# Logits of seven of the eight key heads from float32r halves in three terms, in a one-core attention and feed-forward block

## The reference

```python
q = apply_rope((layernorm(x) @ Wq).reshape(b, t, 32, 128)).reshape(b, t, 8, 4, 128)
k = apply_rope((ctx @ Wk).reshape(b, t, 8, 128))
v = (ctx @ Wv).reshape(b, t, 8, 128)
logits = jnp.einsum('btkgd,bTkd->bkgtT', q, k) * 0.0883883
logits = 30 * jnp.tanh(logits / 30)
weights = softmax(where(mask, logits, -1e30))
x = x + einsum('bkgtT,bTkd->btkgd', weights, v).reshape(b, t, 4096) @ Wo
# then: NF4-quantise and dequantise w1, w2, w3 (blocks of 64)
h = silu(layernorm(x) @ dq1.T) * (layernorm(x) @ dq2.T)
x = x + h @ dq3.T
```

## Time and profile before

| | |
|---|---|
| time, median of 3 runs | 800.66 us (799.59 to 801.32) |
| profiled execution | 800.16 us, of which the span is 798.3 us |
| TensorE busy | 789.0 us, 99% |
| VectorE busy | 661.7 us, 83% |
| ScalarE busy | 547.4 us, 69% |
| GpSimd busy | 367.3 us, 46% |
| granted TensorE clock | 9 (full) in all 40 slices |

### The profile page before, as it was taken

One profiled execution on the slowest core, in us unless ns is written; L12 is line 12 of the kernel. 1 busy time (PEld: TensorE's weight loads), 2 busy tenths in 40 slices (PEclk: granted clock), 3 DMA queues, 4 the chain that ended last, 5 costly groups with the idle time before them and its releaser, 6 DMA issues.

```text
span 798.3 us, 10879 instructions
## 1 busy us (share of the span) xinstructions
PE 789.0 (99%) x3810; PEld 635.9 (80%) x3810; DVE 661.7 (83%) x741; ACT 547.4 (69%) x859; POOL 367.3 (46%) x210
## 2 busy tenths in 40 slices
PE   8999999999999999999999999999999999999998
PEld 6777887878887788878888888888778888888876
DVE  6897755898999999898988889899574999999913
ACT  6467737787877868678787788786643877868510
POOL 4773265446637457366465365473100534435010
PEclk9999999999999999999999999999999999999999
DMA  9636456333432433425235335231401031412022
GB/s 335 199 129 201 131 155 169 110 99 93 139 107 77 154 97 112 129 71 171 79 84 152 92 93 165 80 103 47 136 14 40 27 126 54 124 28 76 14 69 106
DMA packets 60981, 87.56 MB, mean 110 GB/s; under 512 B 6272, under 2 KB 29952, under 8 KB 60928
## 3 DMA queue, kind: packets, MB, share of 16 engines
q1 hardware_dynamic: 59744, 84.06, 35.7%
q10 hardware_dynamic: 1184, 2.82, 1.0%
HBM read 51.00 MB, written 19.07 MB: 88 GB/s over the span
## 4 chain that ended last, share of the span: by engine, by line
PE 85%; DVE 6%; issue 5%; ACT 2%; DMA 1%; POOL 0%; POOLq 0%; SPq 0%; DVEq 0%
PE bank L530 7%; PE prjs L514 7%; PE prjs L516 7%; PE bank L532 7%; PE bank L531 7%; PE prjs L515 7%; PE bank L590 7%; PE avp L618 6%; PE trp L503 4%; PE bank L496 3%; PE bank L498 3%; PE bank L497 3%; PE prjs L498 2%; PE prjs L496 2%; PE prjs L497 2%
## 5 line engine op out<-in xcount | busy, mean ns | idle before, releaser
L1294 POOL TENSOR_TENSOR qT<-cs_loop,sw 128x512 f32<-128x512 f32 x56 | 107.2, 1915 | 183.4 <-DMA sw<-cs_loop 176.1
L514 PE MATMUL prjs<-xh,wqh 128*128 128x512 f32 x256 | 123.3, 482 | 0.0
L530 PE MATMUL bank<-woh,ath 128*128 128x512 f32 x256 | 100.8, 394 | 1.0 <-DVE atl L1161 0.9
L516 PE MATMUL prjs<-xh,wql 128*128 128x512 f32 x256 | 100.2, 391 | 0.0
L532 PE MATMUL bank<-woh,atl 128*128 128x512 f32 x256 | 99.9, 390 | 0.0
L531 PE MATMUL bank<-wol,ath 128*128 128x512 f32 x256 | 99.7, 389 | 0.0
L862 ACT ACTIVATE ath<-trp 128x512 fp32r<-128x512 f32 x64 | 38.2, 596 | 89.5 <-PE trp L503 89.5
L515 PE MATMUL prjs<-xl,wqh 128*128 128x512 f32 x256 | 99.5, 389 | 0.0
L995 DVE TENSOR_TENSOR cs_loop<-prjs,csq 128x1024 f32<-128x1024 f32 x56 | 68.3, 1220 | 21.4 <-PE prjs L516 21.2
L987 DVE SCALAR_TENSOR_TENSOR nfv<-nfq,nfv 128x1408 f32<-128x1408 uint8 x42 | 79.1, 1883 | 0.2
L850 ACT ACTIVATE nrm<-avp,rs 128x128 f32<-128x128 f32 x256 | 72.6, 372 | 7.0 <-DVE rs L1148 6.7
(11 more groups left out here) (187 smaller groups left out, 1966.6 us busy)
## 6 DMA issues: line engine op xcount, KB each, us to landing
sw<-cs_loop SPq DMA_DIRECT2D x112, 128.0 KB, 2.3
stage<-wq_pieces SPq DMA_DIRECT2D x32, 256.0 KB, 2.9
stage<-wo_pieces SPq DMA_DIRECT2D x32, 256.0 KB, 3.1
stage<-dq_scratch SPq DMA_DIRECT2D x32, 256.0 KB, 3.2
ks_scratch<-qT SPq DMA_DIRECT2D x16, 256.0 KB, 3.1
vs_scratch<-vst SPq DMA_DIRECT2D x16, 256.0 KB, 3.5
kcur<-ks_scratch SPq DMA_DIRECT2D x16, 256.0 KB, 2.9
vcur<-vs_scratch SPq DMA_DIRECT2D x16, 256.0 KB, 3.4
```

What stands on the lines that cost most here:

```text
L514: nc.tensor.matmul(o, wqh[:, g, k, :], xh[:, k, cs], start=k == 0, stop=False)
L516: last = nc.tensor.matmul(o, wql[:, g, k, :], xh[:, k, cs], start=False, stop=k == KT - 1)
L530: nc.tensor.matmul(o, ah, wh[:, g, :], start=g == 0, stop=False)
L1294: nc.gpsimd.tensor_tensor(dst, products(ru, slot)[:, 0, :], sw[:, slot, :], ALU.add).then_inc(roped, 1)
```

## The change

For key heads 1 to 7 (steps 8 to 63) the logits are made in three terms of float32r. Head 0 keeps float32, with its operands now in the tiles `kfirst` and `qfirst`. For every unit u from 8 on:

- GpSimd's `query_rope` writes the rotated query back into `cs_loop` (`roped_query(u)`) and not into `qT`;
- ScalarE makes its high part (`query_high`, into `qT`, now float32r), between exp and `high`;
- VectorE makes its low part (`query_low`, into `ql`), between `mask` and `rope_parts`.

The keys of the next head are loaded into `kraw`; ScalarE copies the high part to `kcur` in steps b = 2 and 6 (`key_high`) and GpSimd subtracts for the low part `klow` in steps b = 3 and 7 (`key_low`). `rope_parts` waits for the low part of the unit that held its slot. Tiles are placed anew, and a DMA scratch size is given to the builder.

```diff
             def logits(j):
...
-                if s == 0:
-                    pe.wait_ge(roped, NK + 8 * kv + 4 * h + 4)
-                    pe.wait_ge(k_in[h], 16 * kv + 16)
+                if s == 0 and kv == 0:
+                    pe.wait_ge(roped, NK + 4 * h + 4)
+                    pe.wait_ge(k_in[h], 16)
+                if s == 0 and kv > 0:
+                    pe.wait_ge(q_low_done, 8 * kv + 4 * h - 4)
+                    pe.wait_ge(k_low_done, 2 * kv + h - 1)
                 wait(pe, weights_done, j)
-                nc.tensor.matmul(lgp[:, :], kcur[:, h, s * 128:(s + 1) * 128],
-                                 qT[:, h, :, s * 128:(s + 1) * 128], start=True, stop=True).then_inc(logits_done, 1)
+                if kv == 0:
+                    nc.tensor.matmul(lgp[:, :], kfirst[:, h, ss], qfirst[:, h, :, ss],
+                                     start=True, stop=True).then_inc(logits_done, 1)
+                else:
+                    three(lgp[:, :], [(kcur[:, h, ss], klow[:, h, ss], qT[:, h, :, ss], ql[h][:, :, ss])])\
+                        .then_inc(logits_done, 1)
...
+            def query_high(u):
+
+                kv, half, g = unit_parts(u)
+                act.wait_ge(roped, NK + u + 1)
+                act.wait_ge(logits_done, 8 * (kv - 1) + 4 * half + 4)
+                nc.scalar.activation(qT[:, half, g, :], roped_query(u), ACT.Copy).then_inc(q_high_done, 1)
+
+            def key_high(kv, h):
+
+                act.wait_ge(k_in[h], 16 * kv + 16)
+                nc.scalar.activation(kcur[:, h, :], kraw[:, h, :], ACT.Copy).then_inc(k_high_done, 1)
...
                     if j + 3 < NSTEP:
                         weights(j + 3)
+                    if 8 <= j + 7 < NUNIT:
+                        query_high(j + 7)
                     if j + 2 < 8 * NKV - 8:
                         high(34 + j)
                     if j + 1 < NSTEP:
                         values(j + 1)
+                    if b in (2, 6) and not last:
+                        key_high(kv + 1, b // 4)
...
                 dve.wait_ge(proj_done, ru + 1)
-                wait(dve, roped, ru - 1)
+                if ru < NK + AHEAD + 2:
+                    dve.wait_ge(roped, ru - 1)
+                else:
+                    dve.wait_ge(q_low_done, ru - NK - AHEAD - 1)
...
+            def query_low(u):
+
+                kv, half, g = unit_parts(u)
+                dve.wait_ge(q_high_done, u - 7)
+                nc.vector.tensor_tensor(ql[half][:, g, :], roped_query(u), as_f32(qT[:, half, g, :]), ALU.subtract)\
+                    .then_inc(q_low_done, 1)
...
                     if j + 3 < NSTEP:
                         mask(j + 3)
+                    if 8 <= j + 7 < NUNIT:
+                        query_low(j + 7)
                     u = j + AHEAD
                     if u < NUNIT:
                         rope_parts(NK + u, u % 2, csq[:, :, :])
...
                 if u < 8:
                     pool.wait_ge(k_out[u], 32)
-                else:
-                    pool.wait_ge(logits_done, 8 * (kv - 1) + 4 * half + 4)
-                rope(NK + u, u % 2, qT[:, half, g, :])
+                rope(NK + u, u % 2, qfirst[:, half, g, :] if u < 8 else roped_query(u))
+
+            def key_low(kv, h):
+                pool.wait_ge(k_high_done, 2 * kv + h - 1)
+                nc.gpsimd.tensor_tensor(klow[:, h, :], kraw[:, h, :], kcur[:, h, :].bitcast(f32),
+                                        ALU.subtract).then_inc(k_low_done, 1)
...
+                    if b in (3, 7) and not last:
+                        key_low(kv + 1, b // 4)
                     if j + 2 < 8 * NKV - 8:
                         weight_low(34 + j)
                     if j + AHEAD < NUNIT:
...
-    nc = bacc.Bacc("TRN2", target_bir_lowering=False, num_devices=1)
+    nc = bacc.Bacc("TRN2", target_bir_lowering=False, num_devices=1, dynamic_dma_scratch_size=4096)
```

More of the change, by code:

```diff
@@ L98, in build @@
             wgl = sb("wgl", [128, 2, 2, KT, 128], f32r, ffn)
-        kcur = sb("kcur", [128, 2, 512])
+        with ExitStack() as first_head:
+            kfirst = sb("kfirst", [128, 2, 512], f32, first_head)
+        kcur = sb("kcur", [128, 2, 512], f32r)
         vcur = sb("vcur", [128, B, DH + 1])
@@ L103, in build @@
         eb = sb("eb", [128, 2, 512])
-        qT = sb("qT", [128, 2, G, 512])
+        with ExitStack() as first_head:
+            qfirst = sb("qfirst", [128, 2, G, 512], f32, first_head)
+        qT = sb("qT", [128, 2, G, 512], f32r)
         with ExitStack() as ffn:
@@ L127, in build @@
             nfx = sb("nfx", [128, CH], f32, loop)
+            ql0 = sb("ql0", [128, G, 512], f32r, loop)
         sb("ffn_place", [128, 6144])
@@ L136, in build @@
         wol1 = sb("wol1", [128, G, D], f32r)
+        ql1 = sb("ql1", [128, G, 512], f32r)
+        with ExitStack() as arriving:
+            kraw = sb("kraw", [128, 2, 512], f32, arriving)
+        klow = sb("klow", [128, 2, 512], f32r)
+        ql = [ql0, ql1]
         woh, wol = [woh0, woh1], [wol0, wol1]
@@ L177, in build @@
                                                     sem("h_lo"))
+        q_high_done, q_low_done = sem("q_high_done"), sem("q_low_done")
+        k_high_done, k_low_done = sem("k_high_done"), sem("k_low_done")
         mask_step, key_swapped = sem("mask_step"), sem("key_swapped")
@@ L209, in nf_stored, with roped_query @@
             return 32 + 16 * c if c <= NKV else 32 * (c - NKV) + 32 + 16 * NKV
+        def roped_query(u):
+            return cs_loop[:, u % 2, 0, :]
         def products(ru, slot):
@@ L354, in k_store @@
                 wait(sp, roped, u + 1)
-                sp.dma_start(ks_d[u % 8, u // 8], qT[:, u % 8 // 4, u % 4, :]).then_inc(k_out[u % 8], 16)
+                sp.dma_start(ks_d[u % 8, u // 8], qfirst[:, u % 8 // 4, u % 4, :]).then_inc(k_out[u % 8], 16)
             def head_piece(p):
@@ L389, in _ @@
                     wait(sp, consts, 2)
-                    sp.dma_start(kcur[:, 0, :], ks_d[0, 0]).then_inc(k_in[0], 16)
+                    sp.dma_start(kfirst[:, 0, :], ks_d[0, 0]).then_inc(k_in[0], 16)
                     sp.dma_start(vcur[:, 0:4, 0:DH], vs_d[0, 0]).then_inc(v_in[0], 16)
@@ L419, in head @@
                         wait(sp, logits_done, j + 3)
-                        sp.dma_start(kcur[:, b // 4, :], ks_d[kv + 1, b // 4]).then_inc(k_in[b // 4], 16)
+                        sp.dma_start(kraw[:, b // 4, :], ks_d[kv + 1, b // 4]).then_inc(k_in[b // 4], 16)
                     for c in nf_finished(j - 1):
@@ L441, in weights_in @@
                 sp.dma_start(stage[:, n % 4, :], dq12[:, col:col + D]).then_inc(piece_in[n % 4], 16)
-            sp.dma_start(kcur[:, 1, :], ks_d[0, 1]).then_inc(k_in[1], 16)
+            sp.dma_start(kfirst[:, 1, :], ks_d[0, 1]).then_inc(k_in[1], 16)
             sp.dma_start(vcur[:, 4:8, 0:DH], vs_d[0, 1]).then_inc(v_in[1], 16)
@@ L585, in logits @@
                 kv, h, s = j // B, j % B // 4, j % 4
-                if s == 0:
-                    pe.wait_ge(roped, NK + 8 * kv + 4 * h + 4)
-                    pe.wait_ge(k_in[h], 16 * kv + 16)
-                wait(pe, weights_done, j)
-                nc.tensor.matmul(lgp[:, :], kcur[:, h, s * 128:(s + 1) * 128],
-                                 qT[:, h, :, s * 128:(s + 1) * 128], start=True, stop=True).then_inc(logits_done, 1)
+                ss = slice(s * 128, (s + 1) * 128)
+                if s == 0 and kv == 0:
[4 more added lines that the diff above has]
+                    pe.wait_ge(k_low_done, 2 * kv + h - 1)
+                wait(pe, weights_done, j)
+                if kv == 0:
[4 more added lines that the diff above has]
+                        .then_inc(logits_done, 1)
             for v in range(16):
@@ L1332, in _ @@
                     pool.wait_ge(k_out[u - 8], 16)
-                key_rope(u, qT[:, u % 8 // 4, u % 4, :])
+                key_rope(u, qfirst[:, u % 8 // 4, u % 4, :])
                 if u < 6:
```

## The result

The changed kernel takes 837.99 us (median of 4 runs, 836.49 to 838.81) against 800.99 before: a ratio of 1.0468, 95% interval 1.0455 to 1.048, so 4.7% or 37 us slower. I had predicted 825 us with a range of 803 to 838: the direction and the rough size were right, but a third of the loss was missing, and the median lies at the very edge of the range. In the profiled executions 35.8 of the 38.7 us more fall between the first and the last `rope_parts` of the loop.

The account below looks back on a forecast made before the run. TensorE was taken to set the pace before, and a one-step loop through VectorE after. 24 - 1.9 - 0.7 + 4 = 25.4 us on the profiled 800.16 gave 825 us, range 803 to 838.

Parts of the forecast that it names:

- TensorE's gain: Logits on TensorE: three float32r matmuls replace the float32 call, saving 0.18 us a step, 10 us over 56 steps.
- the closed loop: `rope_parts`, swap, GpSimd's addition, `query_high`, `query_low`, next `rope_parts` form a one-step loop; likeliest case, 815 to 840 us, 74%.
- 7.45 us for a quiet step: Loop length in a quiet step, just under TensorE's 7.48, so lateness from heavy steps is not given back.
- 9.55 for the step with `nf_prepare`: VectorE works without idling in that interval, so its 8.95 us plus the subtraction becomes 9.55.
- the loop's price: Added time over the 55 `rope_parts` intervals from the closed loop: 19 to 28 us, middle 24.
- the lock: VectorE and GpSimd shut each other out of SBUF ports; charged only for 14 `key_low` ahead of `query_low`: 4 us of 0 to 18.
- 24 - 1.9 - 0.7: Loop's loss, less 1.9 us that `atl` may be late before TensorE stops, less 0.7 for steps 57 to 60.
- VectorE's work in it plus 0.60: Between two `rope_parts`, an interval lasts at least VectorE's former work plus the subtraction's 0.60 us.
- the locks pile up: Rival: ScalarE and GpSimd held behind late rotations, and `key_low` at its full 18 us; over 840 us, 5%.
- in a quiet step this costs nothing: ScalarE waiting in `query_high` for the rotation costs nothing in quiet steps, since the rotation is done before exp.
- rival two: VectorE is merely full: lateness is made up in quiet steps, each costing 7.57 to 7.7 us; 797 to 803 us, 12%.

Follow-up runs that it names:

- e8: Changed kernel without the queries' low part (no VectorE subtraction; logits lack that term) and with ScalarE's `query_high` behind its values: 793.93 us.
- e13: Changed kernel with `query_low` at its place but its second input in PSUM, and the mask's signal to TensorE moved to `query_low`: 814.13 us.
- e1: Changed kernel with `query_low` right behind the next unit's `rope_parts` instead of ahead of it, opening the one-step loop: 830.63 us.
- e6: Kernel before plus 56 VectorE subtractions of 128x512 behind the mask, both inputs in SBUF, result unused: 827.12 us.
- e7: Changed kernel with `query_low` behind `rope_parts` and ScalarE's `query_high` behind the values, all terms kept: 828.52 us.
- e3: Changed kernel without the queries' low part (no VectorE subtraction; the second matmul reads the high part again): 801.89 us.
- e14: e13 with `query_low` behind `rope_parts`, so neither one-step loop nor lock: 812.53 us.
- e16: e14 with ScalarE's `query_high` behind the values: 805.96 us.
- e9: Kernel before plus 56 VectorE subtractions of 128x512 ahead of the mask, one input in PSUM, result unused: 804.28 us.
- e2: Changed kernel with GpSimd's dequantisation scalings behind the weight piece of their step instead of ahead of it: 842.42 us.
- e10: Kernel before plus 56 VectorE subtractions of 128x512 ahead of the mask, both inputs in SBUF, result unused: 817.76 us.

## Why the prediction was right and wrong

**Right: TensorE's gain, 10 us.** In e8, with the three matmuls in place, quiet steps take 7.49 us, where they took 7.66; that is the 0.18 us a step. Of the 10 us 6.4 reach the time there (793.9).

**Right in part: the closed loop as a mechanism.** The chain above is it, and VectorE idles ahead of `query_low` 41 times. But undoing the loop gives back 7 us, not 24. I had 7.45 us for a quiet step, it is 7.31 to 7.34; I had 9.55 for the step with `nf_prepare`, it is 9.07. TensorE's waits were to be some 25 us and are 33.7; its share was to be under 97% and is 95%.

**Wrong in size: the loop's price.** Without the lock my sum was 800.16 + 24 - 1.9 - 0.7 = 821.6. e13 is the kernel that this describes, and it takes 814.1: 7.5 us too much. The 55 intervals grew by 14.2 us there, not 24. What I had too high is the term "VectorE's work in it plus 0.60" for the heavy steps: I took VectorE's work from the trace of before, where without the idle time it is 382.7 us in these intervals, part of it waiting for GpSimd. In e13 it is 364.0 without the subtraction, and the steps with `nf_prepare` take 8.7 us where I had 9.55. Whether steps below 7.45 us (six take 6.8) also gave lateness back was not taken apart.

**Wrong: the lock, "I take 4 us".** e13 to the changed kernel is 23.9 us. This is the step that failed. I had the mechanism (the two examples of VectorE and GpSimd shutting each other out), but applied it to the 14 `key_low` alone and gave `query_low` the length of its unhindered like, 0.60 us. It took 65.8 / 55 = 1.20.

For `key_low` the 4 us were right: `query_low` was held up behind ten of them, by 4.4 us in all. What I left out are the scalings, 23.5 us, and the weight pieces, 4.3 us. The scaling that starts at the addition's end stood in the rows of before. `query_low` is released by the addition's end plus one copy of 0.63 us, and whatever waits on GpSimd behind the addition (scaling, `key_low`) starts at the addition's end, so the subtraction arrives just when it has begun. This explains the 14 subtractions over 2 us, of which e1 has one; it is not needed for the lock's price, since e6, with no such release, pays 1.38 us for each. That the dequantisation is hindered less than before (191.6 to 173.8 us) pays back part.

-7.5 and +19.9 make the 12.4 us between my sum of 825.6 and the 838.0. That the sum came as near as this is in part luck, since the two errors have opposite signs. The rival "the locks pile up" had the right kind of cause at 5%, but for `key_low` at its full 18 us and over 840 us.

**Wrong: "in a quiet step this costs nothing" for ScalarE's wait.** Moving it gave 2 us where other limits are higher (e1 to e7), but 8.0 us (e3 to e8) and 6.6 (e14 to e16) without them. In the changed kernel itself it was not moved.

**Wrong: rival two.** I had "VectorE is merely full" at 797 to 803 us. With the lock, a full VectorE is at 827 (e6) or 831 (e1), nearly the whole loss without any loop. Only without the lock does it come near what I had worked out (e9, 804.3, at TensorE's old step). The two limits, loop and full VectorE, lie 7 us apart with the lock, and this is why the loop's price can't be read from what its removal gives back.

Built up from TensorE's share: 800.2 - 10 = 790.2; to e8 793.9 (+3.7); VectorE's subtraction without lock, e16 806.0 (+12.0); ScalarE's wait early, e14 812.5 (+6.6); the loop, e13 814.1 (+1.6); the lock, 838.0 (+23.9). The sizes hold in this order; another order gives other shares. The +1.6 is not clear of noise, and the +3.7 and +12.0 I did not take apart.

## What to carry to other kernels

Ask of each VectorE instruction to be added whether both of its inputs lie in SBUF: if they do and GpSimd is busy for about half of the time, its unhindered length is too little. Here 0.60 us became 1.06 to 1.38 in the mean and 3.0 at most. Cost it with the rest of the GpSimd instruction that will be under way, or give it an input in PSUM. If it hangs on the end of a GpSimd instruction, look at what GpSimd does next: here that had just begun. And when two limits lie close together, undo them both in a table of four before naming a cause.

## What was unexpected of the hardware

Taking one of 56 identical subtractions' two inputs from PSUM instead of SBUF changed the kernel from 817.8 to 804.3 us with nothing else moved, at a GpSimd that is busy 46 to 47% of the time. In the traces of the changed kernel, e1, e2, e6 and e10 every added subtraction that took over 0.9 us ended 0.54 to 0.56 us after the end of a GpSimd instruction, whichever it was, while one with an input in PSUM ran in 0.69 us beside a scaling of 2.55. And the lock's cost mostly moves and does not vanish: from the changed kernel to e1 VectorE's idle time fell by 19.8 us (35.0 to 15.2), and dequantisation and subtraction together grew by 16.0 (65.8 + 173.8 to 51.7 + 203.9).
